# An attention and mixture-of-experts layer: eight output projection tiles run inside the last head, and the last head's outputs are copied, inverted and multiplied in two column halves

## The reference

```python
xn = layernorm(x)
q, k, v = (heads(xn @ W.T + b) for W, b in ((Wq, bq), (Wk, bk), (Wv, bv)))   # 16 heads of 16
q, k = rope(q), rope(k)
scores = q @ k.T / 4          # only the first 205 and the last 512 keys are allowed, for every query
out = softmax(scores) @ v
attn = out.transpose(...).reshape(2048, 256) @ Wo.T + bo
ffn = expert[top1(xn @ router.T)](xn) * weight      # 8 experts, silu(gate) * up, down
return x + attn + ffn
```

## Time and profile before

| | |
|---|---|
| median of 3 runs | 416.41 us (415.82 to 417.6) |
| profiled execution | 417.95 us, its span 416.1 us |
| TensorE busy | 376.5 us, 90% of the span |
| VectorE busy | 323.8 us, 78% |
| ScalarE busy | 265.0 us, 64% |
| granted TensorE clock, mean of the profiled execution | 0.987 |
| last head, first exponential to last | 384.07 to 397.69 us |
| output projection, first to last matmul | 398.73 to 412.83 us |

### The profile page before, as it was taken

The page is one execution under the profiler, slowest core; times in us unless marked ns, Lnnn a source line. Parts: engine busy times, 40 slices in busy tenths (PEclk is TensorE's granted clock), DMA queues, the critical chain, the costliest instruction groups (busy, mean ns, idle before and its releaser), DMA issues.

```text
span 416.1 us, 12241 instructions
## 1 busy us (share of the span) xinstructions
PE 376.5 (90%) x4646; PEld 189.4 (46%) x4646; DVE 323.8 (78%) x549; ACT 265.0 (64%) x537; POOL 65.7 (16%) x82
## 2 busy tenths in 40 slices
PE   0884989979898999999999999999999999998896
PEld 0553445646565444444444444444444444442265
DVE  5769287797763788888888888878888888884666
ACT  2622255754344677777778777777887777788920
POOL 5005242232200003303123032030000000000000
PEclk9999799999999899999999999999999999999999
DMA  7997244455411211213123032131120210246716
GB/s 250 406 395 167 54 132 142 148 179 169 112 54 51 67 49 47 71 27 93 43 57 89 13 89 66 29 94 33 38 62 20 58 56 17 69 134 99 156 49 205
DMA packets 30920, 42.53 MB, mean 102 GB/s; under 512 B 10724, under 2 KB 25700, under 8 KB 30048
## 3 DMA queue, kind: packets, MB, share of 16 engines
q1 hardware_dynamic: 29000, 36.71, 30.6%
q0 software_dynamic: 1872, 5.11, 4.8%
HBM read 27.75 MB, written 13.67 MB: 100 GB/s over the span
## 4 chain that ended last, share of the span: by engine, by line
PE 77%; DVE 11%; ACT 5%; issue 4%; DMA 3%; SPq 0%; ACTq 0%; DVEq 0%; POOLq 0%
PE ps L714 22%; PE ps L696 20%; PE ps L642 17%; PE ps L589 4%; PE ps L752 3%; PE ps L602 3%; PE ps L541 2%; ACT probs L1251 2%; DMA o_st<-sorted_rows,token_of 2%; PE ps L628 2%; DMA x_sb<-x_in 1%; DVE parts L959 1%; DVE mx L996 1%; PE ps L503 1%; PE ps L497 1%
## 5 line engine op out<-in xcount | busy, mean ns | idle before, releaser
L1002 DVE TENSOR_REDUCE mx<-ps 128x1 f32<-128x717 f32 x232 | 198.9, 899 | 37.4 <-PE ps L642 35.2
L714 PE MATMUL ps<-q_op,k_op 98*32 98x512 bf16 (+1 forms) x1472 | 131.2, 384 | 7.5 <-ACT probs L1251 5.7
L642 PE MATMUL ps<-k_op,q_op 96*32 96x512 bf16 (+1 forms) x1856 | 118.7, 317 | 0.8 <-ACT ys L1218 0.7
L1251 ACT ACTIVATE probs<-ps 128x512 f32<-128x512 f32 x192 | 99.2, 602 | 24.4 <-PE ps L714 24.3
L642 PEld LDWEIGHTS ps<-k_op,q_op 96*32 96x32 bf16 x1856 | 53.8, 96 | 74.1 <-issue 34.9
L714 PEld LDWEIGHTS ps<-q_op,k_op 98*32 98x32 bf16 (+1 forms) x1472 | 40.5, 95 | 64.6 <-ACT probs L1251 25.6
L696 PE MATMUL ps<-probs,v_op 128*32 128x512 f32 x384 | 50.1, 595 | 0.2 <-ACT o_st L1242 0.2
L1251 ACT ACTIVATE dn<-ps 77x512 f32<-77x512 f32 x64 | 34.9, 597 | 10.9 <-PE ps L714 10.9
L1251 ACT ACTIVATE gu<-ps 128x512 f32<-128x512 f32 x64 | 33.0, 602 | 10.6 <-PE ps L714 10.6
L1251 ACT ACTIVATE wqk<-ps 128x512 f32<-128x512 f32 x64 | 33.0, 602 | 10.6 <-PE ps L714 10.6
L445 POOL DMA_INDIRECT o_st<-sorted_rows,token_of x23 | 26.1, 1135 | 82.2 <-PE ps L575 52.5
(11 more groups left out here) (118 smaller groups left out, 371.2 us busy)
## 6 DMA issues: line engine op xcount, KB each, us to landing
q_parts<-parts SPq DMA_DIRECT2D x12, 256.0 KB
sorted_results<-ys SPq DMA_DIRECT2D x23, 128.0 KB
q_op<-q_parts SPq DMA_DIRECT2D x15, 192.0 KB
gu<-gu_in SPq DMA_DIRECT2D x1, 2816.0 KB
tab<-tab_in SPq DMA_DIRECT2D x1, 2048.0 KB, 11.5
sorted_rows<-xn SPq DMA_DIRECT2D x4, 512.0 KB, 7.0
out<-x_sb SPq DMA_DIRECT2D x8, 256.0 KB, 2.4
q_op<-q_parts SPq DMA_DIRECT2D x15, 128.0 KB
```

The source lines that it names most:

```text
L642: ins = pe.matmul(ps[r:r + CW, at + c0:at + c0 + n], q_op[slot][0:KR, P * t + r:P * t + r + CW], k_op[slot][0:KR, c0:c0 + n], start=True, ...
L714: ins = pe.matmul(bank(4 + u % RING)[r:r + w, :], k_op[k][:, c0 + r:c0 + r + w], q_op[k][:, QB * b:QB * b + QB], start=True, stop=True)
L1002: dve.tensor_reduce(mx[:, slot, t:t + 1], ps[:, at:at + NK], AX.X, ALU.max).then_inc(max_reduced, 1)
L1251: act.activation(prob[c][0:rows, QB * b:QB * b + QB], bank(4 + u % RING)[0:rows, :], ACT.Exp, scale=SCALE).then_inc(exp_done, 1)
```

## The change

It gives TensorE eight of the sixteen m = 0 tiles at M places 6 to 13 of head 15, each as four matmuls of 32 weight columns; the other eight m = 0 tiles stay behind the last `pv`. ScalarE copies the last head's bank 7 in two halves of the columns (bank columns 0 to 255 and 256 to 511, so each half holds 256 columns of all four query blocks), VectorE inverts each half by itself, SP issues the output DMAs after both copies and the reciprocal DMAs in eight pieces of 16 rows x 1 KB, and VectorE multiplies eight pieces of 256 columns. A half's pieces wait for all four reciprocal DMAs of the half. Pairs are then projected, added and written in the order 0, 2, 4, 6, 1, 3, 5, 7.

```diff
@@ -61,6 +61,9 @@
 ORDER = 2 * ("MSSMSSMP" + "MSSMSSMP" + "MSSMSSP")
 assert (ORDER.count("S"), ORDER.count("M"), ORDER.count("P")) == (UNITS, NT, NCH)
 ROUNDS = (HEADS - 4) // RING
+EARLY_OUT = 4 * 2
+OUT_SLOTS = {6 + n: n for n in range(EARLY_OUT)}
+PAIRS = [2 * b + half for half in range(2) for b in range(NQB)]
 XR = 4
 EARLY_MAX = 6 * 512
 
@@ -221,7 +224,8 @@
             sem(n) for n in ("scored", "exp_done", "pv_done", "o_copied", "o_stored"))
 
         attn_in = [sem(f"attn_in{n}") for n in range(3)]
-        last_in = [sem(f"last_in{b}") for b in range(NQB)]
+        last_copied, last_o_in = sem("last_copied"), sem("last_o_in")
+        last_recip_in = [sem(f"last_recip_in{n}") for n in range(2)]
         last_inverted = sem("last_inverted")
         sum_stored, sum_in, recip_done, recip_stored = (
             sem(n) for n in ("sum_stored", "sum_in", "recip_done", "recip_stored"))
@@ -407,18 +411,21 @@
             head_step(15, 0, load=False, turn=False)
             load_attn(HEADS - 2, HEADS - 1, attn_in[2])
 
-            sp.wait_ge(o_copied, HEADS)
+            sp.wait_ge(last_copied, 2)
             for b in range(NQB):
                 sp.dma_start(attnT[P - DH:P, HC - 1, QB * b:QB * b + QB],
-                             o_st[0][VW * b:VW * b + DH, :]).then_inc(last_in[b], 16)
-            sp.wait_ge(last_inverted, 1)
-            for b in range(NQB):
-                sp.dma_start(recips[P - DH:P, HC - 1, QB * b:QB * b + QB],
-                             last_recip[VW * b + DH:VW * b + 2 * DH, :]).then_inc(last_in[b], 16)
+                             o_st[0][VW * b:VW * b + DH, :]).then_inc(last_o_in, 16)
+            for half in range(2):
+                sp.wait_ge(last_inverted, half + 1)
+                c0 = QB // 2 * half
+                for b in range(NQB):
+                    sp.dma_start(recips[P - DH:P, HC - 1, QB * b + c0:QB * b + c0 + QB // 2],
+                                 last_recip[VW * b + DH:VW * b + 2 * DH, c0:c0 + QB // 2]
+                                 ).then_inc(last_recip_in[half], 16)
 
             ov = out_d.rearrange("(t p) d -> p t d", p=P)
-            for pair in range(NT // 2):
-                sp.wait_ge(out_ready, pair + 1)
+            for n, pair in enumerate(PAIRS):
+                sp.wait_ge(out_ready, n + 1)
                 sp.dma_start(ov[:, 2 * pair:2 * pair + 2, :], x_sb[:, 2 * pair:2 * pair + 2, :]
                              ).then_inc(out_stored, 16)
             sp.wait_ge(out_stored, 16 * (NT // 2))
@@ -698,6 +705,13 @@
                                     start=c == 0, stop=c == NCH - 1)
                 ins.then_inc(pv_done, 1)
 
+            def out_tile(t, m, r=0, w=P):
+
+                pe.wait_ge(attn_ready, NQB if m else t // 4 + 1)
+                return pe.matmul(ps[r:r + w, HID * t:HID * t + HID], attnT[:, m, P * t + r:P * t + r + w],
+                                 wo[:, HID * m:HID * m + HID], start=m == 0 and t % 2 == 0,
+                                 stop=m == HC - 1, skip_group_check=True)
+
             def head_step(h, k, first=False, rest_of_next=True, start_after=True):
 
                 u = j = p = 0
@@ -722,6 +736,13 @@
                             if j == NT // 2:
                                 pe.wait_ge(qk_loaded, (h + 3) * LOADS)
                             max_tile(h + 2, j - NT // 2, (k + 2) % RING)
+                        if h == HEADS - 1 and j in OUT_SLOTS:
+                            if OUT_SLOTS[j] == 0:
+                                pe.wait_ge(wo_in, 16)
+                                pe.wait_ge(neg_copied, HEADS)
+                                pe.wait_ge(max_reduced, HEADS * NT)
+                            for r in range(0, P, CW):
+                                out_tile(OUT_SLOTS[j], 0, r, CW)
                         if j == NT // 2 + 1 and rest_of_next and not start_after:
                             pe.wait_ge(max_reduced, (h + 2) * NT)
                             turn_neg(h + 1, (k + 1) % RING)
@@ -744,25 +765,16 @@
             head_step(15, 0, rest_of_next=False, start_after=False)
             pv(15, NCH - 1, 0)
 
-
-            def out_tile(t, m):
-
-
-                pe.wait_ge(attn_ready, NQB * m + t // 4 + 1)
-                ins = pe.matmul(ps[:, HID * t:HID * t + HID], attnT[:, m, P * t:P * t + P],
-                                wo[:, HID * m:HID * m + HID], start=m == 0 and t % 2 == 0,
-                                stop=m == HC - 1, skip_group_check=True)
-                if m == HC - 1 and t % 2 == 1:
-                    ins.then_inc(out_proj, 1)
-
-            pe.wait_ge(wo_in, 16)
-            pe.wait_ge(neg_copied, HEADS)
-            for m in range(HC):
-                for t in range(NT):
-                    if m == 0 and t == NT // 2:
-                        pe.wait_ge(exp_done, HEADS * UNITS)
-                        pe.wait_ge(o_copied, HEADS)
-                    out_tile(t, m)
+            pe.wait_ge(exp_done, HEADS * UNITS)
+            for t in range(EARLY_OUT, NT):
+                if t == NT - 2:
+                    pe.wait_ge(last_copied, 2)
+                out_tile(t, 0)
+            for n, pair in enumerate(PAIRS):
+                pe.wait_ge(attn_ready, NQB + n + 1)
+                for t in (2 * pair, 2 * pair + 1):
+                    ins = out_tile(t, 1)
+                ins.then_inc(out_proj, 1)
 
 
         @block.vector
@@ -1110,17 +1122,23 @@
             dve.wait_ge(attn_in[1], 16 * (1 + HEADS // 2 - 2))
             for b in range(NQB):
                 divide(1, 0, P - 2 * DH, b)
-            dve.wait_ge(o_copied, HEADS)
             dve.wait_ge(o_stored, 16 * NQB * (HEADS - 2))
-            dve.reciprocal(last_recip[:], o_st[0][:]).then_inc(last_inverted, 1)
+            for half in range(2):
+                dve.wait_ge(last_copied, half + 1)
+                cols = slice(QB // 2 * half, QB // 2 * half + QB // 2)
+                dve.reciprocal(last_recip[:, cols], o_st[0][:, cols]).then_inc(last_inverted, 1)
             dve.wait_ge(attn_in[2], 32)
-            for b in range(NQB):
-                dve.wait_ge(last_in[b], 32)
-                divide(1, P - 2 * DH, P, b, attn_ready)
+            dve.wait_ge(last_o_in, 16 * NQB)
+            rows = slice(P - 2 * DH, P)
+            for n, pair in enumerate(PAIRS):
+                dve.wait_ge(last_recip_in[n // NQB], 16 * NQB)
+                cols = slice(2 * P * pair, 2 * P * pair + 2 * P)
+                dve.tensor_tensor(attnT[rows, 1, cols], attnT[rows, 1, cols], recips[rows, 1, cols], ALU.mult
+                                  ).then_inc(attn_ready, 1)
 
             dve.wait_ge(y_added, NT)
-            for pair in range(NT // 2):
-                dve.wait_ge(out_proj, pair + 1)
+            for n, pair in enumerate(PAIRS):
+                dve.wait_ge(out_proj, n + 1)
                 both = x_sb[:, 2 * pair:2 * pair + 2, :].rearrange("p t d -> p (t d)")
                 dve.tensor_tensor(both, bank(pair), both, ALU.add).then_inc(out_ready, 1)
 
@@ -1260,7 +1278,11 @@
                     head_step(i * RING + 2 + j, (2 + j) % RING)
             for h in (14, 15):
                 head_step(h, h % RING)
-            copy_o(HEADS - 1, 0)
+            act.wait_ge(pv_done, HEADS * NCH)
+            act.wait_ge(o_stored, (HEADS - 1) * (16 * NQB))
+            for half in range(2):
+                cols = slice(QB // 2 * half, QB // 2 * half + QB // 2)
+                act.copy(o_st[0][:, cols], bank(7)[:, cols]).then_inc(last_copied, 1)
 
 
 # ---- launch: one core; the host only lays data out ----
```

## The result

The changed kernel takes 419.25 us (median of 19 runs, 416.67 to 422.23) against 415.75 for the kernel before in the same sessions (19 runs, 412.03 to 421.82). The ratio is 1.0105, 95% interval 1.0074 to 1.0136: 4.4 us slower, 3.1 to 5.7. Forecast was +3.8 us.

What follows compares the result with a forecast made beforehand. Two limits: head 15 alternates TensorE and ScalarE; behind the last `pv` TensorE sets the end, normalization next at once. 1.8 (head) + 1.5 (last addition) + 0.5 (backlog) = +3.8 us on 416.41 gives 420.2 us; 80% range 417.0 to 422.2.

Steps and rivals of the forecast that it cites:

- Forecast +1.8 us: Head 15: eight early tiles at 0.43 us each, partly absorbed by TensorE's slack, lengthen the head by 1.8 us.
- my stepping: Head 15, order stepped through with three banks: chunk 2 costs nearly nothing, the rest 0.86 each, 1.7 us.
- SP's queue and the wait for four: Tail: reciprocal DMAs queue behind four output DMAs, the first product waits for all four: 405.9 against 404.87 before.
- Rival C: SP issues DMAs every 0.39 us and slack takes the tiles: not slower, 417.1 or 416.1 us; chance 0.18.
- Rival B: Head 15: early tiles cost more than their columns, 0.6 or 0.86 us each; 421.3 or 423.4 us; chance 0.09.
- D: Faster by over 0.5%: Rival C's quick queue and slack in full, landings under 2.0 us; 413.9 us; chance 0.06.
- rival A: Tail: TensorE's clock falls in its new 3.9 us gap and TensorE ends late; 421.1, up to 422 us; chance 0.12.
- the sign "eight additions in a row": Tail: VectorE's eight additions run in a row, ready-made pairs waiting, the last 16.2 us behind the last `pv`.
- the forecast's bound (VectorE and outputs): Tail: VectorE, not TensorE, is late; its additions end at 415.0, then outputs queue with 0.7 us of backlog.
- +1.5 for the last addition: Tail: eight VectorE additions, 0.67 us each, start behind all products at 409.65 and end at 415.0 against 413.54.
- +0.5 of backlog: End of tail: eight output DMAs of 0.77 us come 0.67 us apart, adding 0.5 us of backlog over before.

Runs made afterwards that it cites:

- the six tiles: Changed kernel with six early tiles instead of eight, all at M places between two pairs of score blocks; ratio 1.0051 to the kernel before.
- the gap filled: Changed kernel with its eight late m = 0 tiles computed twice, to fill TensorE's gap; ratio 1.0108 to the kernel before.
- the split alone: Changed kernel without its early tiles, all sixteen m = 0 tiles behind the last `pv`; ratio 1.0053 to the kernel before.
- the own-block kernel: Changed kernel with eight semaphores for the reciprocal DMAs, each product waiting only for its own block and half; ratio 1.0057 to the kernel before.
- the two queues: Changed kernel with a semaphore per reciprocal DMA and the last head's four output DMAs issued from ScalarE's queue; ratio 1.0066 to the kernel before.
- the early tiles alone: Kernel before plus the eight early tiles; copy, reciprocal, DMAs and products unsplit; ratio 1.0053 to the kernel before.
- the four kernels with additions between products: The split alone with additions between products (1.0032), the combined kernel (0.9955), it without the split (1.0009), it without early tiles (1.0001).
- the unsplit kernel: The combined kernel with copy, reciprocal, reciprocal DMAs and products whole, in four blocks of 512; ratio 1.0009 to the kernel before.
- the combined kernel: Changed kernel with six early tiles between score blocks, semaphore per DMA, ScalarE's queue for outputs and second-half reciprocals, additions between products; ratio 0.9955 to kernel before.

## Why the prediction was right

**Early tiles in the head: the price right, the slack put wrong.** Forecast +1.8 us, measured +2.16. A tile at 0.43 us was right, and so was 0.86 for each of chunks 3 and 4. The term that was too small is chunk 2: my stepping had both of its tiles nearly free, but it grew by 0.43. The traces of the changed kernel and of the six tiles show the rule for this loop: five of the eight places lie directly before or behind a `pv`, in the loop exponential, score block, `pv`, score block, and cost 0.43 each (5 x 0.43 = 2.15); three lie between score blocks and cost nothing.

**SP's queue and the wait for four: right.** The first product was forecast 7.0 us behind the copy (405.9 - 398.87) and came at 403.61 - 396.61 = 7.00; the second half at 9.43 against 406.04 - 396.61 = 9.43. The price of a 1 KB-row DMA that I had taken from the whole one was right (0.589 both). The Trainium skill, "DMA: Bandwidth & Descriptors", section "Measured (HBM→SBUF, 128 partitions, SWDGE, issued from GpSimd)", calls transfers under 64 KB descriptor-dominated. The issue times here agree with that, though the page measured transfers of another kind and not their issue: 0.589 us for 16 KB and for 32 KB. Rival C had its condition against it: none of SP's twelve issues was under 0.58 us, and the slack took three of eight tiles. Rival B fell with the 0.43 us of a tile, D with C.

**The clock: rival A's event and path, and its small price.** I had the fall as likely and mostly harmless in time, and that it was. It fell after gaps of 3.90, 3.16, about 3.0 and 2.39 us of the tail, and not after 2.05 or less. But the forecast named the wrong engine for the end. In the profiled execution of the changed kernel TensorE came last (the last four additions wait 0.17 us each for it, as before), and the last addition ended 413.68 - 396.47 = 17.2 us behind the last `pv`, not 16.2; the sign "eight additions in a row" didn't come. A had 1.3 us as the cost of the low clock on m = 1; it was 1.7. With the gap filled, VectorE came last as forecast, and the tail was the same within 0.2 us. So the forecast's bound (VectorE and outputs) and A's bound lie at the same height, and removing one uncovers the other. That they do was not worked out beforehand: that the time agrees in spite of the other path is in part luck.

**The additions and the outputs: the term mis-sized.** Forecast +1.5 for the last addition and +0.5 of backlog. In the trace with the clock up (the split alone) it is 15.78 - 14.67 = +1.1 and 3.8 - 2.56 = +1.2, in sum 2.3 against 2.0: the additions run 0.60 us apart, not 0.67. The 0.67 was misread: the row of four (2.68 us) contains the whole duration of the last (0.69) and a wait of 0.18 us: the fourth addition starts at 409.40, held up by TensorE, where 0.60 behind the third would have been 409.21. In the changed kernel itself, with the low clock, it is +2.4 and +0.1. The split's cost in time, 2.2 us (0.7 to 3.7), agrees with the sum.

**The sum.** 2.16 + 2.46 = 4.6 by the trace, 4.4 by the times of many runs, against 3.8. The miss of 0.6 is 0.4 in the head and the rest in the tail.

## What to carry to other kernels

Slack of an engine isn't a sum that work can be poured into: in this loop of two engines, an insertion was free only outside the segment that runs from the wait's end to the instruction that feeds the other engine. Work taken from the tail of the engine that bounds it is worth only the distance to the next path, here 0.3 us, so read that distance before moving anything. The split in halves paid here, together with six early tiles and by about 1 us, only once the DMAs that it doubles, their queue and the waits behind them were split with it and the gap in TensorE's work was closed; in the tail, gaps of 2.39 us and more brought the clock down. And a row of several instructions holds their waits: take a price from the spacing of single ones.

## What was not expected

The last 2 MB of output take 6.2 us at 340 GB/s, and in the changed kernel, the one before, the split alone, the filled gap, the own-block kernel, the six tiles and the two queues the span ended 7.96 to 8.08 us behind the issue of the first output DMA. Where the outputs came further apart it was longer: 9.1 us with the early tiles alone, 9.65 to 10.3 in the four kernels with additions between products. The kernel before sits on this bound and on TensorE's at once; I take that as the reason why most single edits to its tail only lose, without having tested it. The clock also fell after a gap as short as 2.39 us (the unsplit kernel), and single executions of one kernel differ by up to 10 us (412.03 to 421.82 before). Most of that is the clock: among the 35 executions of the kernel before that were timed beside the combined kernel, time and mean granted clock correlate with -0.84, some 3.5 us for each 0.01 of mean clock. The three at 1.0 took 407.51 to 408.14 us, the one at 0.982 took 415.63.
